# A graph network block on one core: the second layer norm's output split before it is transposed, and transposed by DMA

## The chip, the cores and the metric

The kernel runs on one core of a Trainium2 chip. A core has a matrix engine (TensorE, here PE), a vector engine (VectorE, DVE), a scalar engine (ScalarE, ACT), a general engine (GpSimd, POOL) and a sync engine (SyncE, SP) which in this kernel only issues DMAs. Each engine works through its own instructions in order and waits at semaphores for the others. The metric is the device time of one execution in microseconds (us); lower is better.

## The reference: two layers over 32 graphs

Each of the 32 graphs has 256 nodes with 512 features. The first layer is a normalised, masked attention with 16 heads of width 32; the second is a normalised single attention whose softmax runs along the other axis. Both add to the residual.

```python
h = jnp.maximum(_layernorm(x), 0.0)
q, k, v = heads(h @ Wq + bq), heads(h @ Wk + bk), heads(h @ Wv + bv)
scores = jnp.where(mask == 0, -inf, einsum('bhqd,bhkd->bhqk', q, k) * scale)
x = x + (einsum('bhqk,bhkd->bhqd', softmax(scores), v)) @ Wo + bo      # layer 1
h = jnp.maximum(_layernorm(x), 0.0)
output, q, k = h @ weight, h @ wq, h @ wk
alpha = jnp.maximum(einsum('bno,bmo->bnm', q, k), 0.0) * (graph != 0)
alpha = softmax(alpha, axis=1)
x = x + einsum('bnm,bmo->bno', alpha, output)                          # layer 2
```

## The kernel before: a software pipeline of 16 steps per graph

All matrix products are done in f16 with each operand split into a high and a low half (`_hi`, `_lo`), three products for one. Splitting takes two instructions: ACT writes the high half, DVE writes what is left. For the second layer the two weight matrices are multiplied ahead of the loop into one (`wm`), so that it needs g = wm·h, al = g·h (the scores), hw = h·w and av (weights times hw).

A body of the loop has 16 steps, one per head. The loop runs bodies -1 to 32, of which bodies 2 to 29 are one hardware loop, and in body t several graphs are in work: the first layer of graph t, the end of the first layer and the second layer of graph t-1, the first products of graph t+1. The table `DENSE` (line 26 on) names the dense products of each step: qk0 to qk3, v0, v1 (projections), ot (transposes of the heads' output), wo (output projection), h2_0 and h2_1 (transposes of the second norm's output), g, al, hw, av. A name with `a` or `b` behind it is half a product. `ROLE` says which graph a name works on, `BANK` which of three PSUM banks it writes. Within a step each engine runs a fixed list: PE begins with `weigh(s-1)`, the product of head s-1's probabilities with the values, then the dense products of the step, then at steps 3, 7, 11, 15 the scores of four heads (`scores`).

A head's probabilities pass through five engines: mask and minimum (DVE, `mask`), exponential (ACT, `exponentials`, three steps ahead of s), high half (ACT, `probs_high`, two ahead), low half (POOL, `probs_low`, two ahead), transpose by DMA (SP, `transpose_probs`, one ahead), and then PE's `weigh` one step after its own number. So in step 5 SP issues the transpose of head 6, and PE needs it at the start of step 7. SP also issues the transposes of the first norm's output of the next graph (`transpose_h1`, step 6), the store, and the loads of the adjacency.

The second norm: PE ends `wo1b` in step 3. DVE adds the result to `x1` and takes statistics (L963, L883), aggregates (L889) in step `VAR2` = 4, ACT takes the root (L698, L701), DVE refines it (L907 to L911) and writes the normalised `work` (L916), 256 nodes in two halves. In step 5 PE transposes `work` by eight f32 matmuls against the identity (L518) between the two halves of v1; ACT applies the relu and writes `h2_hi` (L649), DVE writes `h2_lo` (L921), both transposed already. g0 in step 6 is the first to read them.

Ahead of the loop the scales of the weights are found (`raw_top`, `find_scale`), the weights are split, and in body 0 PE merges the second layer's weights (`merge`, `merged_low`), each with a maximum over all weights that goes through a transpose on PE.

Of the kernel before, what the change touches and what calls it, by code (L numbers as in the profile page):

```python
# [8 lines left out]
P = 128  # L9
# [6 lines left out]
EPS = 1e-5  # L16
# [28 lines left out]
RING = 3  # L45
# [20 lines left out]
BANK = {"qk2": 0, "wo0": 1, "ot1": 2, "wo1": 2, "qk3": 0, "v1": 1, "h2_0": 2, "h2_1": 0, "g0": 2,  # L66
        "g1": 0, "hw0": 1, "qk0": 2, "al": 0, "ot0": 1, "qk1": 2, "hw1": 0, "v0": 1, "av0": 0,
        "av1": 2}
assert sorted(BANK) == sorted(tile(name) for name in ORDER)


ROLE = {"v1": 0, "ot1": -1, "qk2": 0, "wo0": -1, "wo1": -1, "qk3": 0, "h2_0": -1, "h2_1": -1,
        "hw0": -1, "g0": -1, "g1": -1, "hw1": -1, "qk0": 1, "al": -1,
        "av0": -1, "av1": -1, "qk1": 1, "ot0": 0, "v0": 1}
for name in ORDER:
    if name.endswith("a"):
        first = next(s for s, names in enumerate(DENSE) if name in names)
        ROLE[name] = ROLE[tile(name)] + (first > step_of(tile(name)))
        ROLE[tile(name) + "b"] = ROLE[tile(name)]
AL_STEP = step_of("al")  # L80

STATS1, ROOT1, NORM1, LATE_MASK = (8, 9), 10, 12, 5
XA_STEP, SCALE_STEP = 5, 6
HIGH1_STEP, LOW1_STEPS, TURN1_STEP = 14, (0, 2), 6
VAR2 = 4

X1_STEP, XIN_STEP, KEEP_STEP, FAR_STEP = 1, 4, 4, 11
ADJ_STEP, STORE_STEP = 0, 1


SPARE = [tile(name) for name in ORDER if tile(name) in ("hw0", "hw1", "g0", "g1", "al", "av0")]
# [5 lines left out]
SPLIT_TURN = ("wq", "wk", "wv", "wo", "wm", "w1")  # L97
TOP_STEP = 5
LAST_SCALE_STEP = step_of(SPARE[-1])


SPLIT_AT = {(0, 14): 6, (0, 15): 7, (1, 2): 8, (1, 3): 9, (1, 6): 10, (1, 7): 11}
assert len(SPARE) == KT + 2 and TOP_STEP + 4 < LAST_SCALE_STEP
# [11 lines left out]

def bank_before(name, t):

    at, shift = ORDER.index(name), 0
    while True:
        at -= 1  # L120
        if at < 0:
            at, shift = at + len(ORDER), shift - 1
        other = ORDER[at]
        if BANK[tile(other)] != BANK[tile(name)]:
            continue
        graph = t + shift + ROLE[other]
        if t + shift == 0 and tile(other) in SPARE:
            return other, -1 - t
        if t + shift < -1:
# [5 lines left out]
def two_layers(nc, x, adj, adj_t, wq, wk, wv, wo, bq, bk, bv, bo, w1, wq1_t, wk1_t, out):  # L135
# [10 lines left out]
    with ctx:  # L146
# [6 lines left out]
        def sem(name):  # L153
# [83 lines left out]
        h1_in = sem("h1_in")  # L237
# [12 lines left out]
              ("qk", "v", "score", "pv", "ot", "wo", "h2", "g", "al", "hw", "av")}  # L250
# [12 lines left out]
        const_ok = sem("const_ok")  # L263
# [14 lines left out]
                   "h2_0": (lo["h2"], 2, 0), "h2_1": (lo["h2"], 2, 1),  # L278
                   "g0": (lo["g"], 2, 0), "g1": (lo["g"], 2, 1), "al": (l1_masked, 1, 0),
                   "hw0": (lo["hw"], 2, 0), "hw1": (lo["hw"], 2, 1),  # L280
                   "av0": (final, 2, 0), "av1": (final, 2, 1),
                   "qk0": (lo["qk"], 4, 0), "qk1": (lo["qk"], 4, 1),
# [15 lines left out]
        def split_parts(c):  # L298

            slot, half = SPLIT_TURN[c // 2], c % 2  # L300
# [34 lines left out]
        def _(sp):  # L335

            sp.dma_start(xa[:], x_v[0, :, :, :]).then_inc(xa_in, 16)
            sp.dma_start(bias_q[:], bq).then_inc(small_in, 16)
# [3 lines left out]
            for name in LOADS[:EARLY // 2]:  # L342
                for half in range(2):
# [885 lines left out]
```

## Time and profile before

| | |
|---|---|
| time, median of 3 runs | 1570.23 us (1569.32 to 1573.28) |
| the profiled execution's own time | 1570.8 us |
| span of the profile | 1569.0 us |
| PE busy | 1504.6 us, 96%, 16561 matmuls |
| DVE / ACT / POOL busy | 1247.9 / 1128.3 / 1064.8 us |
| mean granted TensorE clock | 0.992 |
| DMA | 226.28 MB, 656198 packets |

PE's matmuls are pipelined, so a matmul's own length is more than the distance to the next; distances between starts tell what it costs. What a step costs is read from the start of one `weigh` (L483) to the next.

### The profile page before, as it was taken

How to read it: one execution, taken by the hardware profiler on the slowest of the kernel's cores; microseconds unless marked ns; L12 is line 12 of the kernel's file. 1: busy time of each engine (PE TensorE's matmuls, PEld its weight loads, DVE VectorE, ACT ScalarE, POOL GpSimd, SP SyncE). 2: the span in 40 equal slices, each digit the busy share in tenths (PEclk: the TensorE clock that was granted, in tenths of full speed). 3: DMA queues.
4: the chain of work that ended last, by engine and by line, in shares of the span. 5: the costliest groups of instructions: out<-in, count | busy, mean ns of one | idle time of the engine just before them, and what ended most of it. 6: DMA issues, size and time to landing. Idle time of an engine off the chain costs nothing.

```text
span 1569.0 us, 50846 instructions
## 1 busy us (share of the span) xinstructions
PE 1504.6 (96%) x16561; PEld 1106.7 (71%) x16561; DVE 1247.9 (80%) x4042; ACT 1128.3 (72%) x2477; POOL 1064.8 (68%) x1478
## 2 busy tenths in 40 slices
PE   2889999999999999999999999999999999999996
PEld 1557777777777777777777777777777777777753
DVE  6778888887887878788888878888887888888763
ACT  2567777777777777777777777777777777777761
POOL 2466767777677777767677776777776777777650
PEclk9999999999999999999999999999999999999998
DMA  7647777667667766666776766777676677767760
GB/s 241 135 95 132 133 163 160 152 136 152 138 138 166 160 144 143 144 136 148 166 157 141 152 140 134 154 160 159 135 158 136 133 161 160 153 135 159 125 119 16
DMA packets 656198, 226.28 MB, mean 144 GB/s; under 512 B 611488, under 2 KB 627872, under 8 KB 656160
## 3 DMA queue, kind: packets, MB, share of 16 engines
q1 hardware_dynamic: 636848, 188.57, 59.1%
q10 hardware_dynamic: 19312, 37.23, 8.5%
q8 instruction: 21, 0.34, 0.1%
q14 instruction: 17, 0.14, 0.0%
HBM read 57.94 MB, written 16.78 MB: 48 GB/s over the span
## 4 chain that ended last, share of the span: by engine, by line
POOL 35%; issue 34%; PE 22%; DVE 4%; ACT 2%; DMA 1%; POOLq 1%; SPq 0%; ACTq 0%; DVEq 0%
PE ring L408 18%; POOL wv_raw L1115 16%; POOL heads_out L1149 6%; POOL x L1172 4%; POOL keep L1181 3%; POOL far L1190 3%; POOL xa L1137 1%; PE score L464 1%; PE pv L483 1%; DMA turned<-wv_raw 1%; POOL newton L1133 1%; PE ring L518 1%; PE pv L485 0%; DVE wk_raw L864 0%; DVE tops L785 0%
## 5 line engine op out<-in xcount | busy, mean ns | idle before, releaser
L1115 POOL TENSOR_TENSOR wv_raw<-wk_raw,wv_raw 128x512 f16<-128x512 f32 x512 | 608.0, 1190 | 362.8 <-ACT wv_raw L638 358.5
L625 ACT ACTIVATE wk_raw<-wk_raw,least 128x256 f32<-128x256 f32 x1024 | 459.0, 497 | 6.8 <-DVE least L864 6.8
L864 DVE CUSTOM_DVE_ANT_0 wk_raw<-score,far,undo_score 128x256 f32<-128x256 f32 x1024 | 444.0, 478 | 7.1 <-issue 5.1
L638 ACT ACTIVATE wv_raw<-wk_raw 128x512 f16<-128x512 f32 x512 | 320.5, 626 | 8.6 <-issue 4.5
L483 PEld LDWEIGHTS pv<-val,turned 128*128 128x128 f16 x2048 | 149.7, 97 | 67.4 <-issue 43.9
L483 PE MATMUL pv<-val,turned 128*128 128x65 f16 x2048 | 185.9, 192 | 10.8 <-DMA turned<-wv_raw 7.0
L408 PE MATMUL ring<-wv_hi,h 128*128 128x256 f16 x1024 | 189.3, 273 | 0.0
L408 PE MATMUL ring<-h,wq_hi 128*128 128x256 f16 x1024 | 176.3, 274 | 7.6 <-DVE wk_lo L827 7.6
L1149 POOL TENSOR_TENSOR heads_out<-o_sum,o_rcp 128x64 f32<-128x64 f32 x512 | 153.0, 320 | 42.6 <-DVE o_sum L879 42.6
L485 PE MATMUL pv<-val,turned 128*128 128x33 f16 x2048 | 178.1, 179 | 0.0
L408 PE MATMUL ring<-h,wk_hi 128*128 128x256 f16 x1024 | 176.6, 274 | 0.0
L485 PEld LDWEIGHTS pv<-val,turned 128*128 128x128 f16 x2048 | 136.1, 96 | 15.3 <-issue 1.3
L408 PE MATMUL ring<-h_hi,wm_hi 128*128 128x256 f16 x512 | 140.4, 274 | 2.0 <-DVE h_lo L921 1.6
L408 PE MATMUL ring<-h_hi,wm_lo 128*128 128x256 f16 x512 | 140.6, 275 | 0.0
L408 PE MATMUL ring<-h,wq_lo 128*128 128x256 f16 x512 | 140.5, 274 | 0.0
L408 PE MATMUL ring<-h_lo,wm_hi 128*128 128x256 f16 x512 | 140.5, 274 | 0.0
L408 PE MATMUL ring<-h,wk_lo 128*128 128x256 f16 x512 | 140.4, 274 | 0.0
L408 PE MATMUL ring<-wv_lo,h 128*128 128x256 f16 x512 | 140.0, 273 | 0.0
L408 PEld LDWEIGHTS ring<-h,wq_hi 128*128 128x128 f16 x1024 | 93.4, 98 | 24.5 <-DVE wk_lo L827 7.7
L408 PEld LDWEIGHTS ring<-wv_hi,h 128*128 128x128 f16 x1024 | 100.2, 98 | 14.2
L464 PE MATMUL score<-stage 32*128 32x256 f16 x3072 | 107.4, 270 | 1.7 <-DVE stage L942 1.2
L939 DVE SCALAR_TENSOR_TENSOR stage<-ring,bias_q,stage 128x256 f16<-128x256 f32 x128 | 61.6, 481 | 58.5 <-ACT stage L660 54.8
(151 smaller groups left out, 3570.6 us busy)
## 6 DMA issues: line engine op xcount, KB each, us to landing
xin<-x_dram ACTq DMA_DIRECT2D x32, 512.0 KB, 3.8
out_dram<-xo SPq DMA_DIRECT2D x32, 512.0 KB, 3.7
xa<-x_dram ACTq DMA_DIRECT2D x31, 512.0 KB, 4.2
adj_in<-adj_dram SPq DMA_DIRECT2D x32, 256.0 KB, 2.9
turned<-wv_raw SPq DMA_TRANSPOSE x512, 3.2
adjt_in<-adj_t_dram SPq DMA_DIRECT2D x32, 256.0 KB, 3.1
wq_raw<-wq_dram SPq DMA_DIRECT2D x2, 512.0 KB, 7.0
wk_raw<-wk_dram SPq DMA_DIRECT2D x2, 512.0 KB, 8.6
```

The source lines that it names most:

```text
L408: last = nc.tensor.matmul(dst, a, b, start=(k == 0 and s == 0), stop=(k == tiles - 1 and s == 2))
L464: last = nc.tensor.matmul(score[i][:, q * NODES:(q + 1) * NODES], stage[rows, g % 2, of_q, q * P:(q + 1) * P], stage[rows, g % 2, of_k, :] ...
L483: nc.tensor.matmul(pv4[:, slot, 0:VCOLS], turned[:, u % DEEP, q, 0, k, :], val[:, k, u, 0:VCOLS], start=(k == 0), stop=False)
L485: last = nc.tensor.matmul(pv4[:, slot, HEAD:VCOLS], turned[:, u % DEEP, q, 1, k, :], val[:, k, u, HEAD:VCOLS], start=False, stop=(k == QT ...
L625: last = nc.scalar.activation(probs[:, at, q, :], probs[:, at, q, :], ACT.Exp, bias=least[:, at, q:q + 1], scale=-1.0)
L638: nc.scalar.activation(halves[:, at, :, 0, :], probs[:, at, :, :], ACT.Copy).then_inc(hi["p"], 1)
L864: last = nc.vector.tensor_tensor_reduce(out=probs[:, at, q, :], in0=score[u % GROUP][:, q * NODES:(q + 1) * NODES], in1=far[:, q, :], scal ...
L939: nc.vector.scalar_tensor_tensor(out=stage[:, k % 2, 1, :], in0=src[:, 0:NODES], scalar=bias_q[:, k:k + 1], in1=stage[:, k % 2, 0, :], op0 ...
L1115: nc.gpsimd.tensor_tensor(halves[:, at, :, 1, :], probs[:, at, :, :], halves[:, at, :, 0, :], ALU.subtract).then_inc(lo["p"], 1)
L1149: last = nc.gpsimd.tensor_tensor(dst, o_sum[:, pair % 2, q:q + 3:2, :], o_rcp[:, pair % 2, q:q + 3:2].unsqueeze(2).broadcast_to([P, 2, HEAD]),
L1172: last = nc.gpsimd.tensor_tensor(x1[:, q, :], xin[:, q, :], out_bias[:], ALU.add)
L1181: last = nc.gpsimd.tensor_scalar(keep[:, q, :], adjt_in[:, q, :], 0, 0, ALU.is_equal, ALU.is_equal)
```

## The change: where the second norm's output is split and transposed, and when the second attention runs

- The PE transposes h2_0 and h2_1 go out of the table. In step 4 ACT writes the relu of `work` to a new tile `half2` (high), two instructions of 128x512, and DVE writes the low half (`second_half` on both). In step 5 SP issues two DMA transposes from `half2` to `h2` (`transpose_h2`), ahead of that step's transpose of head 6.
- av0 and av1 move from steps 14 and 15 to step 6 of the next body, so they work on graph t-2 (`ROLE` -2). The residual for them is kept by a DMA `xo <- x1` issued by SP in step 12 (`keep_residual`), and `xo` is added to in place.
- v1 is one piece in step 5; g0 moves to steps 7 and 8, g1 to 8 and 9, hw0 to 10 and 11, al to step 12, hw1 to 14 and 15; the softmax to step 13; the first norm of the next graph but one to step 13 on POOL and its relu to step 15 on ACT; the store to step 8. g and hw take the room of `wk1_t`'s raw tile.
- Ahead of the loop: wq is loaded right after x, wk from ACT's queue; graph 0's norm is done by DVE; PE starts qk0a when wq alone is split; eight warm-up matmuls; the merges and the scales are spread over more steps (`JOBS`), the splits of wo, w1 and wm over bodies 0 and 1.
- The last bodies have tables of their own (`DENSE_LAST`, `DENSE_END`): ot0 of graph 31 at step 13, and at the end al, then hw0, hw1, then av2 and av3.

```diff
-    ["v1a", "h2_0", "h2_1", "v1b"],
-    ["g0"],
-    ["g1a"],
-    ["g1b", "hw0a"],
-    ["hw0b", "qk0a"],
-    ["qk0b", "ala"],
-    ["alb", "ot0"],
-    ["hw1"],
+    ["v1"],
+    ["av0", "av1"],
+    ["g0a"],
+    ["g0b", "g1a"],
+    ["g1b", "qk0a"],
+    ["qk0b", "hw0a"],
+    ["hw0b", "ot0"],
+    ["al"],
     ["qk1"],
-    ["v0a", "av0"],
-    ["av1", "v0b"],
+    ["v0a", "hw1a"],
+    ["hw1b", "v0b"],
 ]
+            def transpose_h2(b):
+                if started(b - 1):
+                    sp.wait_ge(mm["hw"], count(b - 1, 2, 1))
+                    sp.wait_ge(mm["al"], count(b - 1, 1, 0))
+                for q in range(QT):
+                    sp.wait_ge(lo["h2"], count(b, QT, q))
+                    settle(sp, sp_settled)
+                    sp.dma_start_transpose(
+                        h2[:, :, :, q * P:(q + 1) * P].rearrange("p h d n -> p (h d) n"),
+                        half2[:, q, :, :].rearrange("p h d -> p (h d)")).then_inc(h2_in, 16)
...
+                    if s == TURN2_STEP and prev:
+                        transpose_h2(p)
                     head = ahead(s, TURN_AHEAD, t, cur, nxt)
                     if head:
                         transpose_probs(*head)
                     if s == TURN1_STEP and nxt:
                         transpose_h1(n)
+                    if s == KEEP_X_STEP and prev:
+                        keep_residual(p)
...
-                if name.startswith("h2"):
-                    pe.wait_ge(normed[1], count(b, 2, k))
-                    for d in range(KT):
-                        last = nc.tensor.transpose(dst[:, d * P:(d + 1) * P],
-                                                   work[:, k, d * P:(d + 1) * P], ident[:])
...
+            def second_half(q, b):
+                act.wait_ge(normed[1], count(b, QT, q))
+                if started(b - 1):
+                    act.wait_ge(h2_in, count(b - 1, QT, QT - 1) * 16)
+                nc.scalar.activation(half2[:, q, 0, :], work[:, q, :], ACT.Relu
+                                     ).then_inc(hi["h2"], 1)
...
+            def second_half(q, b):
+                dve.wait_ge(hi["h2"], count(b, QT, q))
+                relu_low(half2[:, q, 1, :], work[:, q, :], half2[:, q, 0, :], lo["h2"])
```

SP's queue in body 30 before, which has the same list as a body of the loop; `turned<-wv_raw` is the transpose of one head, `h<-half` of half a first norm:

```order
L377 DMA adj_in<-adj_dram 128x2x256
L381 DMA adjt_in<-adj_t_dram 128x2x256
L355 DMA_TRANSPOSE turned<-wv_raw 128x8x128
L392 DMA out_dram<-xo 128x2x512
L355 DMA_TRANSPOSE turned<-wv_raw 128x8x128 x6
L367 DMA_TRANSPOSE h<-half 128x8x128 x2
L355 DMA_TRANSPOSE turned<-wv_raw 128x8x128 x9
```

The same body in the changed kernel; L414 is the second norm, L403 the first, L391 a head:

```order
L430 DMA adj_in<-adj_dram 128x2x256
L434 DMA adjt_in<-adj_t_dram 128x2x256
L391 DMA_TRANSPOSE turned<-wv_raw 128x8x128 x5
L414 DMA_TRANSPOSE h<-half 128x8x128 x2
L391 DMA_TRANSPOSE turned<-wv_raw 128x8x128 x2
L403 DMA_TRANSPOSE h<-half 128x8x128 x2
L391 DMA_TRANSPOSE turned<-wv_raw 128x8x128
L449 DMA out_dram<-xo 128x2x512
L391 DMA_TRANSPOSE turned<-wv_raw 128x8x128 x5
L422 DMA xo<-x 128x1024
L391 DMA_TRANSPOSE turned<-wv_raw 128x8x128 x3
```

The first five heads of the list are heads 1 to 5. Heads 6 and 7 stood directly behind them and now stand behind the two L414, and four transposes that are not of a head stand among heads 6 to 8, where it was two.

DVE in the loop before, from the normalising instruction on; L939 and L942 are qk3's low halves, L864 a mask, L921 h2's low half:

```order
L916 TENSOR_SCALAR work<-x,meanvar,rstd 128x512 x2
L938 REGISTER_ALU
L939 SCALAR_TENSOR_TENSOR stage<-ring,bias_q,stage 128x256
L942 SCALAR_TENSOR_TENSOR stage<-ring,bias_k,stage 128x256
L858 REGISTER_ALU
L864 ISA wk_raw,least<-score,far,undo_score 128x256
L864 ISA least 128x1
L864 ISA wk_raw,least<-score,far,undo_score 128x256
L864 ISA least 128x1
L921 SCALAR_TENSOR_TENSOR h_lo<-ring,h_hi 128x4x128 x2
```

DVE in the loop of the changed kernel at the same place (L993 is the normalising instruction, L998 the low half of the second norm's output):

```order
L993 TENSOR_SCALAR work<-x,meanvar,rstd 128x512 [waits nstep2]
L993 TENSOR_SCALAR work<-x,meanvar,rstd 128x512
L998 SCALAR_TENSOR_TENSOR half<-work,half 128x512 [waits hi_h2] x2
L1015 REGISTER_ALU
L1016 SCALAR_TENSOR_TENSOR stage<-ring,bias_q,stage 128x256 [waits hi_qk]
L1019 SCALAR_TENSOR_TENSOR stage<-ring,bias_k,stage 128x256
L935 REGISTER_ALU [waits mm_score]
```

The two low halves move ahead of qk3's and of the mask behind it, directly behind the instruction that writes their input, with a wait for ACT between.

## Rows read from the trace of the kernel before

**Rows 1.** Busy time by engine in one stretch: length, busy (count), PEclk, DMA.
```profile
448.00:496.00 48.00, 47.98 (x558) 35.83 (x557) 38.58 (x127) 36.99 (x82) 34.46 (x48) 1.00 0.71 153
```
**Rows 2.** Waits of PE from 400 to 1200 us: total us, times, longest.
```profile
PE pv L483 <- DMA turned<-wv_raw: 0.8, 2, 0.4
```
**Rows 3.** Timeline, ACT, the second norm's root in bodies 2 and 30.
```profile
163.54 0.30 ACT L698 ACTIVATE newton<-meanvar,eps 128x2 f32<-128x2 f32 x1 [2.64 <-DVE meanvar L889]
...
1451.05 0.30 ACT L698 ACTIVATE newton<-meanvar,eps 128x2 f32<-128x2 f32 x1 [2.63 <-DVE meanvar L889]
```
**Rows 4.** Timeline, PE, one body: start, us, line, tiles, count.
```profile
801.03 0.38 PE L408 MATMUL ring<-wo_lo,heads_t_hi 128*128 128x512 f16 x1
801.25 0.38 PE L408 MATMUL ring<-wo_hi,heads_t_lo 128*128 128x512 f16 x1
...
810.17 1.28 PE L518 MATMUL ring<-ident,work 128*128 128x128 f32 x8
811.28 0.27 PE L408 MATMUL ring<-wv_hi,h 128*128 128x256 f16 x1
...
812.59 0.19 PE L483 MATMUL pv<-val,turned 128*128 128x65 f16 x1
...
812.96 0.27 PE L408 MATMUL ring<-h_hi,wm_hi 128*128 128x256 f16 x1
...
815.58 0.19 PE L483 MATMUL pv<-val,turned 128*128 128x65 f16 x1
...
817.20 0.83 PE L464 MATMUL score<-stage 32*128 32x256 f16 x24
817.97 0.20 PE L483 MATMUL pv<-val,turned 128*128 128x65 f16 x1
```
**Rows 5.** Timeline, DVE, the same body.
```profile
808.87 1.08 DVE L916 TENSOR_SCALAR work<-x,meanvar,rstd 128x512 f32<-128x512 f32 x2
...
811.52 1.29 DVE L921 SCALAR_TENSOR_TENSOR h_lo<-ring,h_hi 128x512 f16<-128x512 f32 x2
813.50 0.69 DVE L948 TENSOR_TENSOR val<-ring,val 128x512 f16<-128x512 f32 x1 [0.69 <-ACT val L667]
...
815.01 0.39 DVE L879 TENSOR_REDUCE o_sum<-pv 128x128 f32<-128x256 f32 x1
```
**Rows 6.** Timeline, ACT, the same body.
```profile
809.59 0.62 ACT L638 ACTIVATE wv_raw<-wk_raw 128x512 f16<-128x512 f32 x1
...
813.12 0.39 ACTq L766 DMA_DIRECT2D xa<-x_dram  x1
```
**Rows 7.** Timeline, POOL and SP's queue, the same body: low halves, transposes issued.
```profile
803.70 2.89 POOL L1115 TENSOR_TENSOR wv_raw<-wk_raw,wv_raw 128x512 f16<-128x512 f32 x2
...
803.46 4.68 SPq L355 DMA_TRANSPOSE turned<-wv_raw  x3
...
813.25 3.98 SPq L367 DMA_TRANSPOSE h<-half  x2
...
817.48 2.71 SPq L355 DMA_TRANSPOSE turned<-wv_raw  x2
```
**Rows 8.** Transposes from issue to landing: all 512 of a head; one at 813.25.
```profile
DMA to landing us min/median/max: 3.0/3.2/6.0
...
h<-half SPq DMA_TRANSPOSE x1, 5.1
```
**Rows 9.** Busy time and granted clock in three stretches, columns as in Rows 1.
```profile
101.00:102.00 1.00, 0.00 (x0) 0.00 (x0) 1.00 (x3) 0.97 (x4) 0.83 (x1) 1.00 1.11 211
...
1520.00:1522.00 2.00, 0.20 (x8) 0.09 (x4) 1.32 (x3) 1.65 (x4) 0.28 (x1) 1.00 0.68 131
...
1523.00:1526.00 3.00, 3.00 (x16) 1.35 (x15) 0.75 (x1) 0.00 (x0) 0.38 (x2) 0.50 0.69 51
```
**Rows 10.** Timeline, PE, the first dense product and the last.
```profile
29.43 0.61 PE L408 MATMUL ring<-h,wq_hi 128*128 128x256 f16 x2 [7.61 <-DVE wk_lo L827]
...
1560.72 0.58 PE L408 MATMUL ring<-hw_hi,e_hi 128*128 128x512 f16 x1 [2.48 <-DVE hw_lo L970]
```

More of the change, by code:

```diff
@@ L32 @@
     ["qk3"],
-    ["v1a", "h2_0", "h2_1", "v1b"],
-    ["g0"],
-    ["g1a"],
-    ["g1b", "hw0a"],
-    ["hw0b", "qk0a"],
-    ["qk0b", "ala"],
-    ["alb", "ot0"],
-    ["hw1"],
+    ["v1"],
[6 more added lines that the diff above has]
+    ["al"],
     ["qk1"],
-    ["v0a", "av0"],
-    ["av1", "v0b"],
-]
+    ["v0a", "hw1a"],
+    ["hw1b", "v0b"],
+]
+DENSE_LAST = [[name for name in step if name != "ot0"] for step in DENSE]
+DENSE_LAST[13] = DENSE_LAST[13] + ["ot0"]
+DENSE_END = [[], ["wo0a", "ot1"], ["wo0b", "wo1a"], ["wo1b"], [], [], ["av0", "av1"], ["g0"], ["g1"],
+             [], [], [], ["al"], ["hw0"], ["hw1"], ["av2", "av3"]]
 RING = 3
@@ L113, in started, with deal, bank_of, order @@
     return not (isinstance(graph, int) and graph < 0)
+def deal(t):
+    if isinstance(t, int) and t >= BATCH - 1:
+        return DENSE_LAST if t == BATCH - 1 else DENSE_END
+    return DENSE
+def bank_of(name, b):
+    if isinstance(b, int) and b == BATCH - 1 and ROLE[name] == -1:
+        return BANK_END[name]
+    return BANK[name]
 def bank_before(name, t):
-    at, shift = ORDER.index(name), 0
+    def order(body):
+        return [other for step in deal(body) for other in step if not other.endswith("b")]
+    body, at = t, order(t).index(name)
     while True:
@@ L337, in _ @@
             sp.dma_start(xa[:], x_v[0, :, :, :]).then_inc(xa_in, 16)
+            for half in range(2):
+                load_raw(sp, "wq", half)
             sp.dma_start(bias_q[:], bq).then_inc(small_in, 16)
@@ L444, in merge @@
                                                 stop=(k == KT - 1))
-                else:
-                    for half in range(2):
-                        wait_raw(pe, "wo", half)
-                    for k in range(KT):
-                        last = nc.tensor.matmul(dst[:], bv_wide[:, k, :], raw["wo"][:, k, :],
-                                                start=(k == 0), stop=(k == KT - 1))
                 last.then_inc(merged, 1)
@@ L596, in body @@
                         spread_scale(0, 2, pv)
-                    if nxt and not cur and s == step_of("qk0") - 1:
+                        for _ in range(WARM):
+                            nc.tensor.matmul(ring[1][:, 0:P], ident[:], ident[:], start=True,
+                                             stop=True)
+                    if nxt and not cur and s == step_of("qk0"):
                         turn_tops(1, pv)
-                    if nxt and not cur and s == step_of("qk0"):
-                        spread_scale(1, 1, pv)
                     if s in SCORE_STEPS:
@@ L606, in body @@
                             scores(g, t)
+                    if nxt and not cur and s == SCORE_STEPS[0]:
+                        spread_scale(1, 1, pv)
             for name in ORDER:
-                assert len({bank_before(name, t) for t in range(2, BATCH - 2)}) == 1
+                assert len({bank_before(name, t) for t in range(2, BATCH - 1)}) == 1
             sweep(pe, body)
@@ L766, in body @@
                         act.dma_start(xa[:], x_v[n + 1, :, :, :]).then_inc(xa_in, 16)
+            for half in range(2):
+                load_raw(act, "wk", half)
             act.wait_ge(const_ok, 2)
@@ L1036, in body @@
                         second_normalise(p)
-                    if s == AL_STEP + 1 and prev:
+                    if soften and cur:
                         second_low(p)
+                    if s == VAR2 and prev:
+                        for q in range(QT):
+                            second_half(q, p)
                     if s in STATS1 and later:
@@ L1049, in body @@
                         first_low(1, n)
+                    if soften and not cur:
+                        second_low(p)
                     if s == LATE_MASK and cur:
```

261 lines of the change are left out of this document (152 added, 109 removed).

## The prediction, on record before the changed kernel ran

> **What bounds the kernel now.** I read the page first, then the busy time by stretches, then PE's waits, then one body of the timeline engine by engine, and last the two ends. In a stretch of 48 us in the middle PE is busy for 47.98 us at the full clock of 2.4 GHz [rows 1], and over 800 us of the middle it waited 0.8 us in all [rows 2]. So in the loop PE is the bound, and its own work sets the period: the second norm's root comes at 163.54 us in body 2 and at 1451.05 us in body 30, 28 periods of 45.98 us [rows 3]. A microsecond of PE work taken out of a body is a microsecond gained only as long as nothing else comes to PE late. The prediction is therefore one comparison: what PE no longer does, against the time at which the new, longer way of h2 lets PE go on.
>
> **What goes.** The eight f32 transposes start at 810.17 us and the next matmul at 811.28 us [rows 4]: 1.11 us per body. The other dense products keep their matmuls and change places. PE's own work is then 45.98 - 1.11 = 44.87 us per body. ACT and DVE keep two instructions each of the same size for h2.
>
> **What PE would reach, and when.** I follow the body around 812 us, with all times on the clock of the trace before. weigh(5), at the head of step 6, starts at 812.59 us; without the transposes that is 811.48. Step 6 was weigh(5) and g0's 24 matmuls; g0 starts 0.37 us after weigh(5), and the 24 end in weigh(6) at 815.58, so a 256-column matmul costs 0.109 us. Now 12 of the 512-column ones of av0 and av1 stand there, 0.22 us apart (801.03 and 801.25), some 2.6 us. So PE could start weigh(6), the head of step 7, at 811.48 + 0.37 + 2.6 = 814.45 us [rows 4].
>
> **When head 6 comes.** Its low half is ready on POOL at 803.70 + 2.89 = 806.59 us, and before SP issues its transpose at once: it is the last of the three that end at 803.46 + 4.68 = 808.14 [rows 7]. In the changed kernel SP has the two transposes of h2 ahead of it, and cannot issue anything before they are. Their chain, which up to the end of wo1b and through the norm is as before:
> - DVE writes `work` from 808.87 to 809.95, its first half by 809.41 [rows 5].
> - ACT's relu of 128x512 costs what its other conversion of that size does, 0.62 us [rows 6]: 809.45 to 810.1, the second to 810.65, their starts a little under the length apart.
> - DVE's two low halves of 128x512 took 1.29 us together [rows 5]. The first waits for ACT, 810.12; the second ends at 811.4.
> - SP issues the first about 0.2 us after its half is ready at 810.8, so at 811.0. Two transposes in a row took 2.71 us, and a head's issue is some 1.23 us, so the spacing is 1.48 us [rows 7]. The second goes at 812.5, head 6 at 813.96.
> - From issue to landing a head's transpose took 3.0 us at least and 3.2 in the median; the one issued at 813.25, just behind the load of xa from ACT's queue (813.12), took 5.1 [rows 6, 8]. The load keeps its step, so head 6 at 813.96 meets it too. The bounds are 3.1 and 5.1; I take the middle, 4.1, since the load is issued a microsecond earlier relative to it than there.
>
> Head 6 lands at 818.1 us (817.1 to 819.1) and PE wanted it at 814.45: late by 3.65 us (2.65 to 4.65). Behind the wait stands all of PE's list: g0a, the scores of step 7, every later head. Other waits at the same place end earlier and are covered: av0 needs qk3's low half, which DVE now writes behind h2's and which is done by 812.3; g0a needs the second h2 transpose, issued at 812.5, and stands behind weigh(6) anyway.
>
> **The next places.** SP goes on with head 7, two transposes of h1 and head 8, each 1.48 us behind the other: head 8 is issued at 813.96 + 4 x 1.48 = 819.9 and lands 3.4 us later at 823.3. PE's weigh(8) stands behind weigh(6), 12 matmuls of g0a (1.31), the scores (0.77, from 817.20 to 817.97) [rows 4], weigh(7) and 24 more matmuls (2.62), with 0.24 for each weigh: 818.1 + 5.2 = 823.3. No further wait by this, up to 1.4 us if head 8 takes 4.8. Later heads gain on SP, since a PE step is 2.6 us and more against 1.48. The residual's copy (L422) and the store are two issues in places where SP has room, and the copy has from step 12 to the next body's step 1: nothing on the path.
>
> So a body costs 3.65 more and 1.11 less: +2.54 us (1.54 to 3.54). The h2 transposes and a head 6 are both there in bodies 1 to 31: 31 x 2.54 = +79 us (+48 to +110).
>
> **The clock.** PE would stand still for over 3 us in each body. Before, an idle 1.5 us around 101 us left the clock at 2.4 GHz; two idle microseconds from 1520 on were followed by 1.2 GHz from 1523 to 1526 at least [rows 9]. Such a spell of 3 us delays PE by 1.5, of which the wait for head 8 hides a part. Nothing shows how often it falls here. Bounds 0 and 1.5 per body; I take 0.5, since part is hidden and not each pause need do it: 31 x 0.5 = +16 us (0 to +47).
>
> **The ends.** PE's first product waits until 29.43 us, 7.61 of it for wk's low half [rows 10]. The new start lets PE begin when wq alone is split, so most of that wait goes, and it normalises graph 0 on DVE without the way over POOL; the merges and their maxima no longer stand in one row. I take -9 us: the 7.61 and a little for the rest (bounds -18, some twice of it, and 0, if something else is late there). At the end hw0 and hw1 now cover the softmax, for which PE waited 2.48 us [rows 10], while h2's DMA way is some 3 us longer than PE's: -2 us (-4 to +3). Together -11 us.
>
> **The sum** is made against the profiled execution's own 1570.8 us (span 1569.0), which is 0.6 over the median of the runs: 1570.8 + 79 + 16 - 11 = 1655 us.
>
> **A rule beside the trace.** The eight f32 transposes cost PE 1.11 us, the DMA way 3.0 us at least per transpose [rows 4, 8]. The Trainium skill, "VectorE: DVE Perf Modes", section "Rules for kernel authors", says to transpose 128x128 on TensorE if PSUM will do as the destination; its section "The three transpose paths" puts the DMA path at 1309 ns against 390 ns. By those figures alone the way would be 0.9 us longer per block; that a DMA transpose of eight blocks lands in 3.2 us, less than 8 x 1.3, says the figure is not what counts here.
>
> **The rivals.**
> - *Full gain.* Head 6 and h2 are in time, PE stays without waits: 31 x -1.11 = -34, with the ends 1570.8 - 34 - 11 = 1526 us. For it: SP has time in total, DMA is at 0.71 [rows 1]. Against it: SP's queue is in order, and even with the shortest landing head 6 comes at 817.0. Chance 0.03.
> - *DVE's sum holds weigh(6).* Head 6 is in time, but weigh(6) also waits for o_sum, which ends at 815.40, just ahead of 815.58 before [rows 4, 5]. Between the end of `work` (809.95) and it DVE has the same instructions in another order, 5.45 us with 0.69 idle [rows 5]; with the new wait for ACT it ends at 809.95 + 5.45 - 0.69 + 0.5 = 815.2. PE loses 0.75 of the 1.11: 31 x -0.36 = -11, and 1549 us. It needs a chain shorter by 2 us. Chance 0.07.
> - *SP's order costs nothing, g0a waits for h2.* If head 6 were not held, g0a would wait for the second h2 transpose: 812.5 + 4.1 = 816.6 against 814.45 + 0.24: late by 1.9, net +0.8, 31 x 0.8 = +25, and 1570.8 + 25 - 11 = 1585 us, slower. Chance 0.07.
> - *Worse than forecast.* The load of xa falls on head 6 (landing 5.1), the clock falls in every body, head 8 waits too: 4.65 - 1.11 + 1.2 = 4.7 per body, 31 x 4.7 = +147, 1707 us. Chance 0.2.
> - *The change leaves the time as it is,* since gain and new waits cancel within 0.3%: chance 0.02; the chances below add the overlaps.
>
> The forecast itself has 0.61. What a measurement of this kernel can tell from no change is about 0.3%, 5 us. Slower by more than that: 0.61 + 0.07 + 0.2 = 0.88. Faster: 0.03 + 0.07 = 0.10. Same: 0.02. With every term at its low bound the forecast gives 1570.8 + 48 + 0 - 22 = 1597 us, with every one at its high bound 1570.8 + 110 + 47 + 3 = 1731. All at once is unlikely, so above the range ends at the worse rival, 1708, and below it takes in the rival at 1585: 1583 to 1708.
>
> **What would show it.** In the profile after: PE's matmuls of L518 gone; PE's waits led by L543 for `turned` (DMA), some 3 us per body and 80 to 120 us in all; the period 48 to 50 us by the second norm's root; SP issuing head 6 about 7 us later, relative to the norm, than before; granted clock under 0.99. It is wrong if PE hardly waits for `turned`, if SP issues the two L414 before DVE has `work`, or if the wait is charged to DVE's o_sum. A period under 46 us falsifies it.

## The result: slower by 13%, and the profile after

The changed kernel takes 1779.96 us (1775.05 to 1783.22), the kernel before 1570.38 us on the same chip: a ratio of 1.132 (95% interval 1.130 to 1.135). The forecast was 1655 us, slower, with a range up to 1708: the direction was right and so was the wait that leads the loss, but the size was far too small.

The second norm's root first. Before it comes at 115.84 us in body 1 and at 1536.86 in body 32, 31 bodies of 45.84 us:

```profile
115.84 0.30 ACT L698 ACTIVATE newton<-meanvar,eps 128x2 f32<-128x2 f32 x1 [3.79 <-DVE meanvar L889]
...
1536.86 0.30 ACT L698 ACTIVATE newton<-meanvar,eps 128x2 f32<-128x2 f32 x1 [6.72 <-DVE meanvar L889]
```

After, in the same bodies:

```profile
114.55 0.29 ACT L757 ACTIVATE newton<-meanvar,eps 128x2 f32<-128x2 f32 x1 [3.34 <-DVE meanvar L966]
...
1747.76 0.30 ACT L757 ACTIVATE newton<-meanvar,eps 128x2 f32<-128x2 f32 x1 [6.73 <-DVE meanvar L966]
```

That is 1633.21 us for the 31 bodies, 52.68 each. The loop costs 1633.21 - 1421.02 = +212.2 us, +6.84 per body. The start gains 1.3 us up to body 1's root, and the stretch behind body 32's root is 1.5 us longer (33.6 against 32.1): together with the loop the 212.4 us between the spans, 1781.4 and 1569.0. So the whole loss is in the loop.

Busy time by stretches, columns as in [rows 1]; the first row answers to it, the others follow the pause of one body:

```profile
448.00:496.00 48.00, 44.38 (x484) 32.02 (x472) 37.17 (x123) 33.33 (x74) 31.13 (x45) 0.98 0.64 145
...
921.00:922.00 1.00, 1.00 (x9) 0.79 (x7) 0.00 (x0) 0.91 (x3) 0.81 (x1) 0.68 0.73 142
922.00:923.00 1.00, 1.00 (x9) 0.44 (x11) 0.00 (x0) 0.00 (x0) 0.34 (x1) 0.50 0.95 180
923.00:924.00 1.00, 1.00 (x24) 0.64 (x16) 0.00 (x0) 0.00 (x0) 0.00 (x0) 0.50 1.05 195
924.00:925.00 1.00, 1.00 (x20) 0.67 (x13) 0.11 (x2) 0.00 (x0) 0.00 (x0) 0.62 0.88 170
925.00:926.00 1.00, 1.00 (x12) 0.90 (x10) 1.00 (x5) 0.00 (x0) 0.54 (x2) 1.00 1.13 289
```

PE is no longer busy throughout, and behind its pause the granted clock is at 1.2 GHz for some 3.4 us: the shares missing in four rows, 0.32 + 0.50 + 0.50 + 0.38, are 1.70 us, at half the clock. PE's waits over the whole span (total us, times, longest), where [rows 2] had 0.8 us in the middle:

```profile
PE pv L543 <- DMA turned<-wv_raw: 120.4, 43, 7.3
PE pv L543 <- DVE o_sum L956: 51.8, 32, 2.1
...
PE ring L598 <- POOL heads_out L1247: 15.0, 29, 0.6
PE ring L465 <- DVE stage L1019: 15.0, 29, 0.5
```

A wait of 20.0 us at the start is left out. The four are each there about once per body. Here is that body, whose root is at 909.46 us, 101.91 later than that of [rows 4 to 7]. SP's queue:

```profile
912.89 2.73 SPq L414 DMA_TRANSPOSE h<-half  x2
915.88 3.81 SPq L391 DMA_TRANSPOSE turned<-wv_raw  x2
```

The landing of the head issued at 915.88, from issue, in us:

```profile
turned<-wv_raw SPq DMA_TRANSPOSE x1, 4.5
```

PE, with the four waits in square brackets (start, length, line, tiles; the first stands in step 1, then steps 6, 7 and 15):

```profile
900.57 0.63 PE L598 MATMUL ring<-ident,heads_out 128*128 128x128 f32 x4 [0.51 <-POOL heads_out L1247]
...
914.28 0.60 PE L465 MATMUL ring<-wk_t_raw,e_hi 128*128 128x512 f16 x2 [0.52 <-DVE stage L1019]
...
920.52 0.20 PE L543 MATMUL pv<-val,turned 128*128 128x65 f16 x1 [3.47 <-DMA turned<-wv_raw]
...
920.75 0.38 PE L465 MATMUL ring<-h,wm_hi 128*128 128x256 f16 x2
...
922.85 1.47 PE L524 MATMUL score<-stage 32*128 32x256 f16 x24
924.25 0.23 PE L543 MATMUL pv<-val,turned 128*128 128x65 f16 x1
...
924.60 0.45 PE L465 MATMUL ring<-h,wm_hi 128*128 128x256 f16 x2
...
946.05 0.20 PE L543 MATMUL pv<-val,turned 128*128 128x65 f16 x1 [1.59 <-DVE o_sum L956]
```

From g0a's start to weigh(7) it takes 3.50 us, most of it at the low clock, where 1.31 + 0.77 was due [rows 4]; with weigh(7) itself, 0.35 for 0.24, that is 1.53 us lost. Each wait also costs some 0.16 us beyond its number, since idle time is counted from the modelled end of the last matmul, 0.16 behind the point at which the next could have started. The body then adds up to: -1.11 (transposes) + 3.63 + 0.68 + 1.75 + 0.67 (waits) + 1.53 (clock) = +7.15. From its weigh(0) at 898.38 us to the next at 951.28 it took 52.90 us, 6.90 more than the body of [rows 4] (46.00) and much like the mean (+6.84): the rest of PE's steps are 0.25 us shorter in it than the forecast had them.

These terms are where PE stands still, but not all are costs of their own. av0's 0.68 us lie just ahead of weigh(6), and nothing on head 6's way waits for av0. Without them PE would have come to weigh(6) at 916.21 instead of 916.89 us and would still have gone on at 920.52. So the place costs 4.31 us, the wait for head 6 covers av0's, and only about 0.67, 1.75 and the clock come on top. This is worked out from the times; the run with other banks below bears on it.

The wait of 1.59 us in step 15 comes from DVE's list. The softmax stands there in step 13, one step behind al:

```profile
938.83 0.69 DVE L1058 SCALAR_TENSOR_TENSOR work<-ring,keep 128x512 f32<-128x512 f32 x1 [0.83 <-PE ring L465]
...
941.85 0.17 DVE L1081 TENSOR_SCALAR l_sum<-l_sum 128x2 f32<-128x2 f32 x1 [1.35 <-ACT work L766]
...
943.93 0.88 DVE L1089 SCALAR_TENSOR_TENSOR e_lo<-work,l_rcp,e_hi 128x256 f16<-128x256 f32 x2
...
945.60 0.39 DVE L956 TENSOR_REDUCE o_sum<-pv 128x128 f32<-128x256 f32 x1
```

DVE stands 0.83 us for al's product and 1.35 for ACT's exponential, with two masks, qk's low halves and a head's sum queued behind, and PE's weigh(14) needs the room which that sum frees.

### The profile page after: what moved, and what is told of

It reads as the page before. It is cut to its first block, busy times and chain, and to the rows that moved or that the text cites. A ratio compares the mean times of both kernels' runs of the same rounds, so it can differ in the third digit from the quotient of the medians.

```text
span 1781.4 us, 50712 instructions
## 1 busy us (share of the span) xinstructions
PE 1525.1 (86%) x16324; PEld 1095.4 (61%) x16324; DVE 1268.0 (71%) x4054; ACT 1127.1 (63%) x2477; POOL 1055.2 (59%) x1470
## 4 chain that ended last, share of the span: by engine, by line
issue 45%; POOL 38%; PE 5%; DVE 4%; DMA 2%; SPq 2%; POOLq 2%; ACT 1%; DVEq 0%; ACTq 0%
POOL wv_raw L1213 18%; POOL heads_out L1247 6%; PE ring L465 4%; POOL x L1270 4%; POOL keep L1279 4%; POOL far L1288 3%; POOL xa L1235 3%; DMA turned<-wv_raw 2%; DVE wk_raw L941 1%; SPq L414 1%; POOLq L1212 1%; DVE tops L851 1%; DMA out_bias<-bo_dram 1%; SPq L391 0%; POOL minus_mean L1226 0%
## 5 line engine op out<-in xcount | busy, mean ns | idle before, releaser
L543 PE MATMUL pv<-val,turned 128*128 128x65 f16 x2048 | 189.1, 193 | 173.1 <-DMA turned<-wv_raw 120.4
L465 PE MATMUL ring<-h,wm_hi 128*128 128x256 f16 x1024 | 199.4, 299 | 7.2 <-DMA h<-half 7.2
L465 PE MATMUL ring<-wv_hi,h 128*128 128x256 f16 x1024 | 183.0, 272 | 0.2 <-DVE wv_lo L893 0.2
L465 PE MATMUL ring<-w_hi,h 128*128 128x512 f16 x512 | 174.4, 382 | 6.1 <-DVE heads_t_lo L1032 4.9
L954 DVE RECIPROCAL o_rcp<-pv 128x4 f32<-128x4 f32 x256 | 45.1, 176 | 172.6 <-PE pv L545 172.0
L465 PE MATMUL ring<-h,wm_lo 128*128 128x256 f16 x512 | 152.8, 298 | 0.0
L738 ACT ACTIVATE wk_t_raw<-ring 128x512 f16<-128x512 f32 x64 | 38.2, 597 | 170.0 <-PE ring L465 170.0
L524 PE MATMUL score<-stage 32*128 32x256 f16 x3072 | 116.4, 286 | 4.6 <-DVE stage L1019 4.1
L1047 DVE TENSOR_TENSOR wk_t_raw<-ring,wk_t_raw 128x512 f16<-128x512 f32 x64 | 44.3, 692 | 106.0 <-ACT wk_t_raw L733 105.9
```

The lines of the kernel that those rows point to most:

```text
L465: last = nc.tensor.matmul(dst, a, b, start=(k == 0 and s == 0), stop=(k == tiles - 1 and s == 2))
L524: last = nc.tensor.matmul(score[i][:, q * NODES:(q + 1) * NODES], stage[rows, g % 2, of_q, q * P:(q + 1) * P], stage[rows, g % 2, of_k, :] ...
L543: nc.tensor.matmul(pv4[:, slot, 0:VCOLS], turned[:, u % DEEP, q, 0, k, :], val[:, k, u, 0:VCOLS], start=(k == 0), stop=False)
```

## The experiments

The theory after the result: six costs per body, each with its own place: head 6 behind SP's two new transposes, the clock's fall behind that pause, the softmax too close behind al, the load of xa beside head 6's transpose, the first norm's relu on ACT in step 15, and av0's bank. Rivals: DMA work alone slows everything; or the new order of products is dear by itself. All times are medians; each ratio is against the kernel before on the same chip, with its 95% interval. Before was 1566.72 us beside the first four, 1571.52 beside the next four, 1567.94 beside the last three. The changed kernel itself ran only beside the 1570.38 us above, so a difference to its 1779.96 us also holds the difference between chips, some 4 us for the first four; what the ratios give (against 1.132, times 1570 us, to about 4 us) stands beside it.

**Head 6 first on SP's queue.**

```diff
-                    if s == TURN2_STEP and prev:
-                        transpose_h2(p)
                     head = ahead(s, TURN_AHEAD, t, cur, nxt)
                     if head:
                         transpose_probs(*head)
+                    if s == TURN2_STEP and prev:
+                        transpose_h2(p)
```

> In step 5 SP issues head 6's transpose ahead of the two of the second norm; all else as in the changed kernel. Queue-order theory: head 6 is issued some 7 us earlier, PE's wait for it goes, the clock no longer falls, and what is left at step 7 is the wait for DVE's sum and then g0a's wait for the second h2 transpose, some 1.9 us late. Body 48.5 to 49.5 us instead of 52.9, in all 1640 to 1675 us. Rival (the two extra transposes load the DMA engines, whatever their place): still 1765 to 1785 us, with the wait charged to another transpose.

Measured 1716.55 us, 1.094 (1.091 to 1.097): 63 us less than the changed kernel (60 by the ratios), and 42 us above the expected range. PE's waits:

```profile
PE ring L465 <- DMA h<-half: 58.7, 31, 7.2
PE pv L543 <- DVE o_sum L956: 56.6, 35, 4.4
...
PE pv L543 <- DMA turned<-wv_raw: 10.0, 21, 1.7
```

and g0a in one body:

```profile
889.20 0.47 PE L465 MATMUL ring<-h,wm_hi 128*128 128x256 f16 x2 [1.78 <-DMA h<-half]
```

The wait for `turned` shrinks from 120.4 to 10.0 us: SP's order was its cause. In its place g0a waits for h2 itself, 1.78 us and 0.16 of refill (in the mean of 30 waits (58.7 - 7.2) / 30 = 1.72), which is the size in the prediction's third rival (1.9). So about half of the pause belongs to the length of h2's way, whichever goes first. The clock still falls in part of the bodies: their periods are 50.1 to 50.7 us in one group and 51.4 to 51.9 in another. Two bodies side by side had almost the same pause at g0a, the first with 1.89 us and the second with 1.71:

```profile
941.00:942.00 1.00, 1.00 (x11) 0.90 (x10) 0.00 (x0) 0.00 (x0) 0.35 (x1) 1.00 0.91 175
942.00:943.00 1.00, 1.00 (x27) 0.56 (x25) 0.00 (x0) 0.00 (x0) 0.00 (x0) 1.00 0.92 174
...
992.00:993.00 1.00, 1.00 (x9) 0.46 (x11) 0.00 (x0) 0.00 (x0) 0.00 (x0) 0.50 0.96 178
```

Behind g0a's start (940.83 and 990.94 us) the clock stayed up in the first and fell in the second. The body is 50.6 us in the mean, where 48.5 to 49.5 were expected; the clock is about 1.2 us of it where it fell, and what more the expectation missed stays open. The rival, the load of the DMA engines wherever the transposes stand, falls.

**Work for PE in the pause**, to hold the clock. 24 matmuls of 128x256, whose result is of no use, ahead of weigh(6).

```diff
+                    if s == 7 and prev and cur:
+                        pe.wait_ge(lo["v"], count(t, 2, 1))
+                        for _ in range(24):
+                            nc.tensor.matmul(ring[1][:, 0:NODES], WH["wq"][:, 0, 0:P],
+                                             WH["wk"][:, 0, 0:NODES], start=True, stop=True)
```

> The changed kernel with 24 matmuls of 256 columns more per body at the head of step 7, on constant weights into the bank that g0a overwrites, so that PE works through most of the wait for head 6. They add 2.6 us of PE work that is of no use to the result. Clock theory (the pause makes the clock fall to 1.2 GHz for some 3.3 us in every body and costs 1.5 us): faster by 31 x 1.5 = 46 us, 1725 to 1745 us, granted clock near 0.99 or above. Rival (the fall costs nothing since PE waits for a later transpose anyway): 1775 to 1785 us at a higher clock.

Measured 1754.75 us, 1.120 (1.118 to 1.122), 10 us above the expected range and well below the rival's. The clock over the span is 0.992 as before the change, where the changed kernel had 0.966. The stretch behind weigh(6):

```profile
907.00:908.00 1.00, 1.00 (x20) 0.73 (x21) 0.00 (x0) 0.48 (x2) 0.91 (x1) 1.00 1.10 202
```

So the fall does follow PE's pause, and is worth 25 us net (20 by the ratios), 0.6 to 0.8 per body, less than the 1.53 lost at its place: at full clock weigh(8) comes sooner and waits 0.41 us for head 8, which the slow clock had covered.

**The softmax one step later**, two behind al.

```diff
-SOFTMAX_STEP = AL_STEP + 1
+SOFTMAX_STEP = AL_STEP + 2
```

> The changed kernel with the second attention's softmax at step 14 instead of 13. Theory: DVE sits in step 13 waiting for ACT's exponentials of an al that PE has only just finished, so its sum for weigh(14) comes 1.6 us late in step 15; a step later nothing waits. 31 x 1.6 = 50 us less, 1725 to 1740 us. Rival (DVE is merely full there, the wait moves to weigh(15) or to the next body's first sum): 1765 to 1785 us.

Measured 1724.18 us, 1.100 (1.098 to 1.102): 56 us gone (51 by the ratios), 1.6 to 1.8 per body, for a wait that the trace gave as 1.59 + 0.16. The wait itself:

```profile
PE pv L543 <- DVE o_sum L956: 3.6, 2, 2.1
```

**The load of xa in step 3 instead of 5.**

```diff
-XA_STEP, SCALE_STEP = 5, 6
+XA_STEP, SCALE_STEP = 3, 6
```

> The changed kernel with the load of xa issued at the end of ACT's step 3 instead of step 5, so that its data are through before the second norm's transposes. Contention theory: head 6's 4.6 us from issue to landing fall to 3.2 to 3.5, PE's wait shrinks by 1.1 to 1.4 us per body, 31 x 1.25 = 39 us less, 1735 to 1750 us. Rival (three transposes in a row take that long by themselves): 1775 to 1785 us.

Measured 1733.29 us, 1.106 (1.103 to 1.108): 47 us less (42 by the ratios). SP's queue at head 6 in one body:

```profile
892.00 2.71 SPq L391 DMA_TRANSPOSE turned<-wv_raw  x2
```

PE's weigh(6) in it:

```profile
895.57 0.20 PE L543 MATMUL pv<-val,turned 128*128 128x65 f16 x1 [2.26 <-DMA turned<-wv_raw]
```

PE's waits for heads in all:

```profile
PE pv L543 <- DMA turned<-wv_raw: 84.5, 60, 6.8
```

Here weigh(6) starts 3.57 us behind head 6's issue; in the changed kernel it was 920.52 - 915.88 = 4.64. The load from HBM on ACT's queue, issued 2.0 us ahead of the head, lengthened the transpose by about 1 us: from issue to landing it was 4.5 us and is 3.5 here. The shorter pause also lifted the granted clock to 0.984, and av0's wait grew from 0.5 to 1.0 us.

**The first norm's steps as before.**

```diff
-STATS1, ROOT1, NORM1, LATE_MASK = (8, 9), 10, 13, 5
+STATS1, ROOT1, NORM1, LATE_MASK = (8, 9), 10, 12, 5
-HIGH1_STEP, LOW1_STEPS, TURN1_STEP = 15, (0, 2), 6
+HIGH1_STEP, LOW1_STEPS, TURN1_STEP = 14, (0, 2), 6
```

> The changed kernel with the first norm's scaling and its relu on ACT one step earlier again (steps 12 and 14, as in the kernel before); nothing else. Theory: ot1's 0.5 us wait per body for the normalised heads comes from that relu (1.05 us on ACT in step 15), which delays the low half of probabilities that POOL writes just ahead of the heads; with it go 0.5 and some 0.2 us of refill per body, 31 x 0.7 = 22 us: 1758 us (1750 to 1765), and the 15 us of PE's waits for POOL's heads vanish. Rival: POOL is simply loaded, or something one step further waits instead: the time stays at 1775 to 1783 us.

Measured 1769.8 us (1755.09 to 1776.04), 1.128 (1.124 to 1.131). The wait for POOL's `heads_out` is gone from PE's list, so its cause is shown. A gain in time is not: the interval overlaps that of the changed kernel (1.130 to 1.135), and the median lies between theory and rival. The profiled run took 1755.09 us at a clock of 0.972, the three others 1765.8 to 1776.0 at 0.954 to 0.960, so the lower the clock the longer the run. Why the clock differs from run to run stays open.

**Four edits together**: head 6 first, softmax later, xa earlier, norm steps as before.

> The changed kernel with four edits of order together: SP issues head 6 ahead of the two transposes of h2, the second softmax comes two steps behind the attention logits' product instead of one, xa is loaded in step 3, and the first norm's scaling and relu are a step earlier. Theory (the five waits and the clock are the whole loss): a body keeps PE's own 44.9 us, 0.8 and a refill of 0.2 for g0a's wait for h2, 1.0 and 0.2 for av0's wait for qk3's low half, no fall of the clock: 47.1 us, so 1567 - 3 + 31 x 1.1 = 1598 us (1575 to 1615). Rival: the waits cover each other, so that removing one lets the next grow: the sum of the single gains does not add up, 50 us per body and over 1680 us.

Measured 1631.84 us, 1.039 (1.037 to 1.040), above the expected 1598. By the ratios the single edits had gained 60 + 51 + 42 + 8 = 161 us, together they gain 147: most of the loss was independent, against the rival, but not all. PE's waits:

```profile
PE pv L543 <- DMA turned<-wv_raw: 26.4, 35, 2.0
PE pv L543 <- DVE o_sum L956: 25.4, 32, 4.7
PE ring L465 <- DVE stage L1019: 24.5, 29, 0.9
...
PE ring L465 <- DMA h<-half: 14.0, 29, 7.3
```

A body in the middle is 48.1 us. What the expectation lacked are the first two: 0.6 to 0.7 us for head 8, issued behind h1's two transposes, and 0.6 for o_sum, which stands at weigh(0) in step 1 now and no longer in step 15.

**Other banks for av0 and av1**, and head 2's sum ahead of a mask, on top of the four.

```diff
-BANK = {"qk2": 0, "wo0": 1, "ot1": 2, "wo1": 2, "qk3": 0, "v1": 1, "av0": 0, "av1": 2, "g0": 1,
+BANK = {"qk2": 0, "wo0": 1, "ot1": 2, "wo1": 2, "qk3": 0, "v1": 1, "av0": 2, "av1": 0, "g0": 1,
...
+                    if s == LATE_MASK + 1 and cur:
+                        mask(LATE_MASK + 5, t)
...
-                    if s == LATE_MASK and cur:
-                        mask(s + 5, t)
```

> As the one with four edits of order, and av0 and av1 also change their PSUM banks and the sum of head 2's parts on DVE comes ahead of a mask. Theory: av0 then stands in the bank that is freed by wo1, not behind qk3's low half, and its wait of 1.0 us goes, so a body is 45.8 to 46.3 us: 1560 to 1575 us, at the time before the change. Rival: av1 now waits for the same low half just as long (0.5 to 1 us): 1590 to 1600 us, no gain on the one with four.

Measured 1631.15 us, 1.038 (1.037 to 1.040): no gain, so the theory fell, and the rival's 1590 to 1600 as well. The wait for `stage` is gone, and the others took it over:

```profile
PE ring L465 <- DMA h<-half: 39.3, 32, 6.2
PE pv L543 <- DVE o_sum L956: 33.6, 60, 4.1
```

PE reaches g0a sooner and waits there for h2, 1.0 us instead of 0.2. So a wait just ahead of the place where PE waits for the DMA anyway is no cost of its own. The way from wo1 through the norm, ACT, DVE, SP and the DMA to g0a is a limit of its own.

**The kernel before with two transposes added** ahead of head 6, of data that nothing uses.

```diff
+                    if s == 5 and prev:
+                        sp.wait_ge(hi["h2"], count(p, 2, 0))
+                        if started(p - 1):
+                            sp.wait_ge(spare_in, count(p - 1, 32, 31))
+                        for q in range(QT):
+                            settle(sp, sp_settled)
+                            sp.dma_start_transpose(
+                                spare[:, q, :, :].rearrange("p h n -> p h n"),
+                                WH["wq"][:, 2 * q:2 * q + 2, :].rearrange("p h d -> p (h d)")
+                                ).then_inc(spare_in, 16)
```

> The kernel before, with two more DMA transposes of eight 128x128 blocks on SP's queue ahead of head 6, held until ACT has written h2's first high half; what they write is used by nothing. Theory (SP's queue in order is what costs): they are issued near 811.7 and 813.2 us of the body of rows 4, head 6 at 814.7 instead of 808, landing 4.1 to 4.6 later at 818.7 to 819.3 where PE wants it at 815.6: 3.1 to 3.7 us and 0.2 of refill per body, and where the clock falls 0.8 more: 31 x 3.3 to 4.7, so 1670 to 1712 us. Rival: the cost of the changed kernel comes from its new order of products and not from the queue: under 1600 us. Second rival: more DMA work alone slows the transposes everywhere: waits for turned at many steps and not at the head of step 7 alone.

Measured 1728.04 us, 1.100 (1.098 to 1.102), +156.5 us, 16 us over the expected range. SP's queue in one body:

```profile
889.39 2.62 SPq L392 DMA_TRANSPOSE spare<-wq_hi  x2
892.26 4.13 SPq L357 DMA_TRANSPOSE turned<-wv_raw  x2
```

weigh(6) on PE:

```profile
897.17 0.23 PE L495 MATMUL pv<-val,turned 128*128 128x65 f16 x1 [3.72 <-DMA turned<-wv_raw]
```

The clock behind it (the 0.50 ahead of the DMA share):

```profile
898.00:899.00 1.00, 1.00 (x7) 0.69 (x6) 0.00 (x0) 0.57 (x2) 1.00 (x1) 0.50 1.10 208
```

PE's waits for heads in all:

```profile
PE pv L495 <- DMA turned<-wv_raw: 119.4, 39, 6.0
```

With every dense product at its old place two waited-for transposes on SP's queue bring the same pause at the same weigh, and the same fall of the clock. Both rivals fall: the new order of products isn't needed for it, and there is no wait for heads at many steps (39 waits in 31 bodies, with 10 in the whole of the kernel before). The roots of body 1 and 32 are 1579.3 us apart, 50.95 per body and 5.1 more than before: 3.72 + 0.16 for the wait, the rest, 1.2, at the low clock.

**h1's transposes one step later**, behind head 8, on the four edits and on the variant with other banks.

```diff
-HIGH1_STEP, LOW1_STEPS, TURN1_STEP = 14, (0, 2), 6
+HIGH1_STEP, LOW1_STEPS, TURN1_STEP = 14, (0, 2), 7
```

> As the changed kernel with four edits of order (1631.8 us), and SP issues the two transposes of the first norm's output one step later, behind head 8 instead of ahead of it. Theory: of what is left per body, 0.68 us is weigh(8)'s wait for head 8, which stood behind them (issued at 896.5 us, could be at 893.6); with 0.2 of refill 31 x 0.88 = 27 us go: 1605 us (1600 to 1612). Rival: qk0a, four steps later, now waits for them, or the wait for h2 grows by what weigh(8) no longer waits: 1625 to 1632 us.

> The same step later on top of the variant with other banks for av0 and av1 (1631.2 us), where PE reached g0a 0.9 us sooner and waited 1.0 us for h2's transpose. Theory: the waits for h2 and for head 8 are limits of their own, weigh(8)'s 0.55 to 0.77 and refill go: 1605 us (1600 to 1612), the same as with the old banks, since what bounds both is the way of h2 from wo1 to g0a. Rival: 1590 us or less, if the banks only hid their gain behind head 8.

Measured 1626.13 us, 1.037 (1.034 to 1.040), and 1628.78 us, 1.038 (1.035 to 1.040): the theory fell in both, and so did the rival of 1590 us. The first lies in its rival's range, but what took over is neither qk0a nor h2 alone. There weigh(8) no longer waits, and head 9, now behind the same two transposes and the store, is late instead. SP's queue:

```profile
891.67 2.65 SPq L403 DMA_TRANSPOSE h<-half  x2
894.51 0.43 SPq L449 DMA_DIRECT2D out_dram<-xo  x1
895.21 9.65 SPq L391 DMA_TRANSPOSE turned<-wv_raw  x5
```

weigh(9) on PE:

```profile
899.05 0.20 PE L543 MATMUL pv<-val,turned 128*128 128x65 f16 x1 [0.42 <-DMA turned<-wv_raw]
```

**The kernel before with h2's transposes shortened**, 1.11 us of PE's time to 0.44, with other values in h2: what was there to gain in the old order?

```diff
-                    for d in range(KT):
-                        last = nc.tensor.transpose(dst[:, d * P:(d + 1) * P],
-                                                   work[:, k, d * P:(d + 1) * P], ident[:])
+                    last = nc.tensor.matmul(dst[:, :], WL["wo"][:, 0, 0:P], WL["wo"][:, 0, :],
+                                            start=True, stop=True)
```

> The kernel before, with h2's eight f32 transposes on PE (1.11 us per body) replaced by two f16 matmuls of 128x512 (0.44 us) at the same places; h2's values are then others. It measures what there was to gain. Theory: PE is the bound of a body, so all of 0.67 us is gained, 32 x 0.67 = 21 us: 1550 us. Rival: weigh(6) then waits for o_sum, which ended 0.18 us ahead of it, and only 0.2 to 0.4 us per body are gained: 1558 to 1565 us.

Measured 1562.63 us, 0.996 (0.994 to 0.998). Of 21 us in PE's work 5 were gained, part of it ahead of the loop; the 31 bodies took 1418.1 us in its trace, 3.0 less than in that of before. The rival's size holds, but its cause doesn't. It isn't o_sum: PE waits for h2's own low half and for the room in which h2 is written. On its timeline in one body:

```profile
805.85 0.39 PE L517 MATMUL ring<-wo_lo 128*128 128x512 f16 x1 [0.24 <-DVE stage L941]
...
808.02 0.27 PE L408 MATMUL ring<-h_hi,wm_hi 128*128 128x256 f16 x1 [0.26 <-DVE h_lo L920]
```

0.24 + 0.26 with 0.16 of refill is the 0.67 that was removed. So with the table as it was the gain was hardly there: PE already reached g0 when h2 was just ready, and h2 came as early as it did because PE transposed it in 1.11 us. What the gain is in the new table, where g0 stands a step later, this run doesn't show; there PE's own steps did become 1.36 us shorter (below), and waits took more than that.

## Why the forecast was right in kind and wrong in size

- **The chain to head 6: right on SP, partly luck at PE.** Forecast from before were L414's issue at 811.0 and head 6's at 813.96; on this body's clock (+101.9) that is 912.9 and 915.87. Measured: 912.89 and 915.88. The landing was put at 4.1 us, between 3.1 and 5.1, and came out at 4.5, so PE went on at 920.52 us where 920.0 was forecast. That its wait of 3.63 with refill meets the forecast 3.65 is luck: PE also came half a microsecond later (916.89 for 916.36), held by av0. Both waits together are 4.31.
- **PE's own work: right.** In the body read it is 52.90 less 6.73 of waits and 1.53 of clock, 44.6 us; forecast 44.87.
- **The next places: right here, by luck.** No wait at weigh(8), but because the slow clock covers it: at full clock it is 0.41 us, with xa early 0.3, with four edits 0.68. The forecast took the shorter landing for head 8 and had no reserve.
- **The clock: a term mis-sized.** Taken at 0.5 us per body, with 1.5 as the bound. The fall costs 1.53 at its place in the body read, and 0.6 to 0.8 net by the run with work in the pause. The trace of before had a fall behind two idle microseconds [rows 9]; for a pause of over 3 us in every body the bound was the value to take.
- **The step that failed: "So a body costs 3.65 more and 1.11 less".** The sum followed only SP's queue and PE's way from step 6 to weigh(8), and put every other wait of the body at nothing without following the moved steps. Two waits stand elsewhere. In step 15 PE waits for o_sum behind the softmax, 1.75 us; moving the softmax gave 51 to 56 us back. In step 1 ot1 waits for POOL, 0.67; there the wait went with the edit, and a gain in time isn't shown. Together they are 2.42 us per body. For the softmax the diff told it: al as a whole in step 12, the softmax in step 13. It takes a product, DVE, ACT and DVE again, and DVE's list is in order. The first norm's relu, 1.05 us on ACT, was moved just ahead of the high halves on which POOL waits. Neither was followed beyond its own engine.
- **The rest of the miss.** At head 6 the place costs 4.31 instead of 3.65, mostly since the head came half a microsecond later, and the clock 1.03 more than its 0.5. So 2.42 + 0.66 + 1.03 = 4.11 us were missing in the body read, 31 x 4.11 = 127 us; the loop as a whole was 212 - 95 = 117 above its forecast, since the terms of this body add up to 0.3 us more than the mean of +6.84. "Other waits at the same place end earlier and are covered" held: av0 did wait 0.68 us for qk3's low half, and the wait for head 6 covers it.
- **The ends: -11 us forecast, about 0 measured.** PE's first product does start earlier, at 26.53 instead of 29.43 [rows 10], 2.9 us and not 7.6: it still waited for wq's low half. By the first scores 0.8 us of it are left (36.00 for 36.81), since PE waits 4.11 for the biased low halves. The wait moved to what was next in line. At the end g0 starts 7.94 us behind the root instead of 4.66, since h2 comes by DMA, and only 1.8 of these 3.3 us are won back behind it.
- **The full-gain rival.** In the old table 21 us less of PE's work gave 5, so the measure of 1.11 us per body gained was too high there. For the new table no run has the transposes gone and all waits with them; its best form stays 58 us above the kernel before.
- **The range.** Its top was a rival of +4.7 per body. It held only things at SP and at PE's steps 7 to 9. (By its own terms it is 1707 us, and the range says 1708; nothing hangs on it.) A table that moves most of the products brings waits of its own, and these should have widened it upward.

The Trainium skill, "VectorE: DVE Perf Modes", section "Rules for kernel authors", says to transpose 128x128 on TensorE if PSUM will do as the destination. The runs agree: two DMA transposes put into the kernel before cost 5.1 us per body, where the eight on PE take 1.11 us of its time, though the two there also carry what they do to the heads behind them. What made them dear is what a comparison per block doesn't contain, the queue that they share and the time until they land.

No variant with the whole computation beats the kernel before. The best form of the change, the four edits with h1 later, is 1.037 (1.034 to 1.040), not clear of the four edits alone (1.037 to 1.040).

## What to carry to other kernels

Before work is taken off a saturated engine, ask what that work produces and when: if its reader would otherwise be waiting, the engine's time was cover, and taking it away buys little (5 us of 21 here). A DMA that waits for data, put into an in-order queue, delays all that is behind it; add up for each later entry when it lands against when it is wanted, for as many entries as the crowd lasts. And when a table moves many products, follow each moved step to the next wait on every engine, not only the one at the centre of the change: two waits of 0.67 and 1.75 us, far from that centre, were a third of what the body lost here. A wait just ahead of a longer one is covered by it and shouldn't be added.

## What the runs showed of the hardware

- Behind a pause of 3.5 us on PE the clock fell to 1.2 GHz only when PE was at work again, in the body shown 0.8 us after PE had resumed (0.68 over 921 to 922), and stayed there for 3.4 us. With a pause of 1.89 us in one body it stayed at 2.4 GHz, with one of 1.71 us in the next it fell. With 24 matmuls in the pause, which left a wait of 0.9 us, it stayed at 2.4 GHz.
- A DMA transpose of eight 128x128 blocks issued 2.0 us behind a 512 KB load on another queue landed in 4.5 us, and in 3.5 with the load two steps earlier.
- SP issued such a transpose every 1.4 to 1.5 us when its data were there, so two of them held the next by 3 us. The DMA engines were not idle meanwhile: their share was 0.64 over 48 us in the middle of the loop, but 1.42 and 1.05 in two microseconds of PE's pause:

```profile
917.00:918.00 1.00, 0.05 (x1) 0.00 (x0) 1.00 (x6) 0.88 (x3) 0.87 (x3) 1.00 1.42 279
918.00:919.00 1.00, 0.00 (x0) 0.00 (x0) 1.00 (x2) 0.00 (x0) 0.78 (x1) 1.00 1.05 224
```
